# Non-rotated keys and values from a stacked high/low/high latent in fp32r, small constants moved into the norms' tile

## The chip, the cores and the metric

The program runs on one core of one Trainium2 chip. The metric is the device time of one execution in microseconds (us), the median of the runs. TensorE does the matrix products out of SBUF into PSUM, VectorE and ScalarE move and change data in both memories, GpSimd (POOL in the profile) works on SBUF only, and SyncE issues the DMAs. Each engine runs its own instruction stream, and the streams wait for each other on semaphores.

## The reference, cut to what matters

Eight sequences of 512 rows and 256 columns pass through four blocks, each with a layer norm ahead and a residual around it: an attention with three branches, a spiking feed-forward block, a rotary attention with 16 heads of 16, and a product with the signs of a weight. The change touches the first attention, whose first branch takes its keys and values from a latent of 32 columns:

```
ckv    = _rms(x @ w_ckv, g_kvnorm)                        # 512 x 32
k_nope = (ckv @ w_dk_nope).reshape(B, T, 16, 32)          # keys without rotation
v1     = (ckv @ w_dv).reshape(B, T, 16, 32)               # values
k_rope = _rope((x @ w_krope) / 16)                        # one rotated key for all heads
k1     = concat([k_nope, k_rope])                         # 96 per head
scores = x @ w_imp ; idx = top_k(scores, 64)              # rows of the second branch
gate   = softmax((x @ w_gate).mean(over rows))
```

The queries have 96 columns per head, made from a latent of 96 columns; the two other branches take keys and values from x itself and from the 64 rows with the highest scores.

## The kernel before, in words

The program goes through 16 passes: `(0, s)` is the first attention of sequence s, `(1, s)` the second attention of sequence s, in the order (0,0), (0,1), (1,0), (0,2), (1,1) and so on. A pass (0, s) walks over eight pairs of heads, and each pair over twelve units: a unit is a bank of transposed scores, whose exponentials ScalarE takes (`exponentials`, L1857) and whose product with the values TensorE adds into the `outs` banks (`values`, L1218).

Everything else is woven between the units. Each pair g is prepared in seven pieces (`PIECES`: four `qk`, one `nope`, one `val`, one `sel`). For `qk` and `sel`, VectorE multiplies with the rotation's tables (L1423), GpSimd adds (L1961), TensorE transposes (L1112), ScalarE writes the high part and VectorE the low part, the rest that the high part leaves (L1442). `nope` is the product of the keys without rotation (L1092, each pair), of which ScalarE writes the high part and VectorE the low part (L1413) into `K1`; `val` is the values' product (L1095, every second pair). Both read `CKVT`, a tile of 128 rows in float32 whose first 96 rows are zero and whose last 32 hold the transposed latent, against the matching rows of `WQ`. Scores are then three fp32r products of high and low parts (L1181 to L1183). The row maxima are found ahead, from fp32r products at L1147 and VectorE's passes at L1461 and L1464.

`prologue(n, j)` prepares sequence n while the pass (0, n-1) runs: layer norm, transposes, the small projections, VectorE's products for the rotated key (L1571, L1572, in the upper half of the tile `HN`), GpSimd's power and sum (L1945, L2003), the copy of the score row into `ROW` (ScalarE, L1742), its transposes (L1042), the gate's product (L1048), the root mean squares and scaled latents (L1374 to L1586, in the lower half of `HN`), their transposes (L1055), the copies into `NQT` (ScalarE) and `CKVT` (VectorE, L1590), and the ranking of the score row (L1601 to L1615). For the first sequence these steps run with nothing beside them. L1742 is the helper through which ScalarE makes nearly all its copies.

The order of each engine's instructions is fixed when the program is built: `attention_steps` gives each step a time from tables of numbers (`AFTER`, `START`, `PRO`, `MID_A`, `HEADS` and others), in units of one score unit, and sorts. All engines walk through the same sorted list, each doing its own part of a step. `plan_banks` hands the five `work` banks out in that order and counts the readers of each.

Of the kernel before, what the change touches and what calls it, by code (L numbers as in the profile page):

```python
# [11 lines left out]
F32 = mybir.dt.float32  # L12
# [167 lines left out]
def piece_before(g, m, n):  # L180
# [8 lines left out]
AFTER = [dict(pv=2.67, recip=1.87, scale=3.36, late_recip=2.11, late_scale=4.28, scale_gap=0.93, last_recip=1.54, last_scale=3.37, piece=-2.58, gap=0.66, piece_tr=1.99, max=4.98, max_gap=0.31, mt=1.93, rows=-5.38, kr=0.63, val=3.63),  # L189
         dict(odd=3.2, lead=-5.7, lead_odd=4.55, lead_gap=0.79, lead_mt=2.06, pv=3.12, recip=1.78, scale=6.23, last_recip=0.26, last_scale=4.05, max=-0.18, max_gap=1.03, mt=2.45, piece=32.75, gap=1.06, piece_tr=1.93, kr=38.38, val=0.53)]  # L190
# [5 lines left out]
         ("pro_act", 0, 2, 5.29), ("pro_pe", 0, 1, 6.49), ("pro_act", 0, 3, 6.79), ("pro_act", 0, 4, 8.2),  # L196
         ("pro", 0, 4, 8.69), ("pro_pe", 0, 6, 9.1), ("pro_pe", 0, 2, 9.37), ("pro_pe", 0, 3, 11.19),
         ("pro", 0, 5, 11.73), ("pro_act", 0, 5, 12.42), ("kr", 0, 0, 12.93), ("piece", 0, 0, 14.81),
         ("pro_act", 0, 6, 18.69), ("piece", 0, 1, 19.19), ("pro", 0, 6, 20.19), ("piece_tr", 0, 0, 21.05),
         ("piece", 0, 2, 21.32), ("piece_tr", 0, 1, 21.6), ("pro", 0, 7, 22.8), ("piece", 0, 3, 23.83),  # L200
         ("pro", 0, 8, 24.41), ("piece", 0, 4, 24.92), ("piece_tr", 0, 3, 26.89), ("pro", 0, 9, 28.25),
         ("piece", 0, 5, 30.65), ("piece_tr", 0, 4, 30.82), ("pro_pe", 0, 4, 31.22), ("pro_pe", 0, 5, 31.99),
         ("pro", 0, 10, 32.0), ("pro", 0, 11, 37.09), ("pro", 0, 12, 38.82), ("piece", 0, 6, 42.15),
         ("piece_tr", 0, 6, 43.66)]


def tail_steps(at):
# [6 lines left out]
TAIL = [[("wo_early", 3.17), ("wo_last", 5.37), ("tail_add", 0, 5.37), ("tail_add", 1, 6.02),  # L214
         ("tail_var", 0, 7.32), ("tail_var", 1, 8.25), ("tail_ln", 0, 8.6), ("tail_ln", 1, 9.61),
         ("hT", 3, 0, 9.76), ("hT", 3, 1, 10.98), ("sign", 0, 13.37), ("sign", 1, 13.79)],
        [("wo_early", 6.05), ("wo_last", 6.72), ("tail_add", 0, 6.87), ("tail_add", 1, 6.99),
         ("tail_var", 0, 8.23), ("tail_var", 1, 10.23), ("tail_ln", 0, 10.6), ("tail_ln", 1, 10.86),
         ("hT", 3, 0, 12.01), ("hT", 3, 1, 12.37), ("sign", 0, 12.66), ("sign", 1, 13.47)]]
# [5 lines left out]
PRO = [("pro", 0, 58.63), ("pro", 1, 63.32), ("pro_pe", 0, 74.8), ("pro_act", 2, 75.63), ("pro_pe", 1, 76.0),  # L225
       ("pro_act", 3, 76.46), ("pro", 3, 77.3), ("pro_pe", 6, 77.98), ("pro_act", 4, 78.2), ("pro_pe", 2, 80.26),
       ("pro", 4, 83.26), ("pro_pe", 3, 86.16), ("pro_act", 5, 86.54), ("pro", 5, 86.95), ("pro_act", 6, 87.49),
       ("pro", 6, 87.95), ("pro", 7, 88.64), ("pro", 8, 89.15), ("pro", 9, 90.05), ("pro_pe", 4, 93.36),
       ("pro", 10, 94.51), ("pro_pe", 5, 96.73), ("pro", 11, 97.62), ("pro", 12, 104.7)]
# [19 lines left out]
MID_A = [[("ln", 1, 0, 8.17), ("ln", 1, 1, 9.2), ("hT", 1, 0, 9.72), ("hT", 1, 1, 10.6), ("fc", 0, 0, 11.42),  # L249
# [3 lines left out]


MID_B = [("y", 0, 0, 8.85), ("y", 0, 1, 9.75), ("y", 0, 2, 10.47), ("y", 0, 3, 11.45), ("spike", 0, 0, 20.05),
         ("spike", 0, 1, 20.48), ("spike", 0, 2, 21.01), ("spike", 0, 3, 21.23), ("spike", 0, 4, 22.07),
         ("spike", 0, 5, 22.68), ("var", 2, 0, 23.0), ("y", 1, 0, 36.55), ("y", 1, 1, 36.83), ("y", 1, 2, 39.55),
         ("y", 1, 3, 40.63), ("spike", 1, 0, 44.18), ("spike", 1, 1, 45.5), ("spike", 1, 2, 46.17),
         ("spike", 1, 3, 46.23), ("spike", 1, 4, 46.32), ("spike", 1, 5, 46.8), ("var", 2, 1, 47.06),
# [6 lines left out]
         ("fc", 0, 1, 1.52), ("fc", 0, 2, 2.7), ("fc", 0, 3, 3.76), ("y", 0, 0, 5.48), ("y", 0, 1, 6.38),  # L266
         ("y", 0, 2, 6.89), ("y", 0, 3, 7.77), ("spike", 0, 0, 8.65), ("spike", 0, 1, 8.72), ("spike", 0, 2, 8.96),
         ("spike", 0, 3, 9.35), ("spike", 0, 4, 9.8), ("spike", 0, 5, 10.11), ("var", 2, 0, 10.35),
         ("y", 1, 0, 14.35), ("y", 1, 1, 15.12), ("y", 1, 2, 16.02), ("y", 1, 3, 16.66), ("spike", 1, 0, 17.75),
         ("spike", 1, 1, 17.99), ("spike", 1, 2, 18.77), ("spike", 1, 3, 18.79), ("spike", 1, 4, 19.12),  # L270
# [6 lines left out]
          ("heads", 0, 0, 83.62), ("stack", 2, 0, 84.73), ("heads", 1, 0, 85.66), ("stack", 3, 0, 85.93),  # L277
          ("heads", 2, 0, 86.12), ("stack", 0, 1, 86.92), ("heads", 3, 0, 88.26), ("stack", 1, 1, 88.63),
          ("heads", 0, 1, 96.28), ("stack", 2, 1, 96.31), ("heads", 1, 1, 96.88), ("stack", 3, 1, 97.27),
          ("heads", 2, 1, 99.32), ("heads", 3, 1, 100.09), ("v", 0, 100.63), ("v", 1, 106.63)],  # L280
         [("clear", 0, -24.69), ("clear", 1, -19.0), ("stack", 0, 0, -17.57), ("stack", 1, 0, -17.53),
          ("heads", 0, 0, -16.75), ("stack", 2, 0, -16.54), ("heads", 1, 0, -14.38), ("stack", 3, 0, -14.32),
          ("heads", 2, 0, -14.01), ("stack", 0, 1, -13.91), ("heads", 3, 0, -11.88), ("stack", 1, 1, -9.6),
          ("v", 0, -11.26), ("v", 1, -10.97), ("heads", 0, 1, -8.14), ("stack", 2, 1, -7.34),
          ("heads", 1, 1, -5.14), ("stack", 3, 1, -3.83), ("heads", 2, 1, -1.96), ("heads", 3, 1, 3.95)]]


PROJ = [[("proj_early", 5.17), ("proj_last", 7.26), ("proj_add", 0, 7.65), ("proj_add", 1, 7.95),
        ("var", 1, 0, 8.9), ("var", 1, 1, 8.94)],
        [("proj_early", 4.27), ("proj_last", 6.62), ("proj_add", 0, 6.69), ("proj_add", 1, 6.83),  # L290
        ("var", 1, 0, 7.13), ("var", 1, 1, 7.88)]]


def attention_steps(layer, s):

# [153 lines left out]
def plan_banks():  # L449
# [5 lines left out]
    def prologue(n, j):  # L455
        for name in (["hT0", "hT1"], ["small0", "small1"], ["score_cols", "gate"], ["nqT", "ckvT"],
                     ["pos"], ["selT"], ["imp"])[j]:
            work.use(("pro", n, name))
# [103 lines left out]
def build_program(nc, x, w_small, w_imp, w_q, w_nv, w_kw, w_sel, w_proj, g_q, g_kv,  # L562
# [1566 lines left out]
```

## Time and profile before

| | us |
|---|---|
| median of 3 runs | 3019.16 |
| lowest, highest run | 3018.69, 3020.45 |
| profiled execution, its own time | 3020.62 |
| its span | 3018.8 |
| TensorE busy (95% of the span) | 2854.8 |
| VectorE busy (65%) | 1956.6 |
| ScalarE busy (50%) | 1503.6 |
| GpSimd busy (32%) | 957.6 |

The profile is of one execution. Busy times are sums of instructions; matrix products are pipelined, so the time of one is read best from its start to the start of the next. A bracket at the end of a timeline row says how long the engine stood idle ahead of it and which instruction released it. Mean granted TensorE clock is 0.982 of full speed.

### The profile page before, as it was taken

How to read it: one execution, taken by the hardware profiler on the slowest of the kernel's cores; microseconds unless marked ns; L12 is line 12 of the kernel's file. 1: busy time of each engine (PE TensorE's matmuls, PEld its weight loads, DVE VectorE, ACT ScalarE, POOL GpSimd, SP SyncE). 2: the span in 40 equal slices, each digit the busy share in tenths (PEclk: the TensorE clock that was granted, in tenths of full speed). 3: DMA queues.
4: the chain of work that ended last, by engine and by line, in shares of the span. 5: the costliest groups of instructions: out<-in, count | busy, mean ns of one | idle time of the engine just before them, and what ended most of it. 6: DMA issues, size and time to landing. Idle time of an engine off the chain costs nothing. (4 is left out here: it accounts for less than half of the span.)

```text
span 3018.8 us, 53729 instructions
## 1 busy us (share of the span) xinstructions
PE 2854.8 (95%) x18384; PEld 2035.9 (67%) x18384; DVE 1956.6 (65%) x6243; ACT 1503.6 (50%) x3228; POOL 957.6 (32%) x1764
## 2 busy tenths in 40 slices
PE   6999899999999999999999999999999999999987
PEld 4666676667766677666776667766677666776654
DVE  5666656775677656866567766667566775665654
ACT  2554344564445644465444664456544465445543
POOL 1233233432334313333133332334222332233332
PEclk7999999999999999999999999999999999999998
DMA  3111001000110001100101001110111100110000
GB/s 124 34 33 27 25 26 40 25 18 19 41 40 25 25 29 35 33 20 25 38 26 33 25 19 38 33 35 16 30 34 33 31 16 26 33 33 12 16 12 29
DMA packets 58701, 91.44 MB, mean 30 GB/s; under 512 B 19904, under 2 KB 32704, under 8 KB 58176
## 3 DMA queue, kind: packets, MB, share of 16 engines
q1 hardware_dynamic: 58432, 88.01, 9.9%
q8 instruction: 149, 2.44, 0.3%
q14 instruction: 120, 0.98, 0.1%
HBM read 81.68 MB, written 5.24 MB: 29 GB/s over the span
## 5 line engine op out<-in xcount | busy, mean ns | idle before, releaser
L1857 ACT ACTIVATE PR<-work 128x512 f32<-128x512 f32 (+1 forms) x1088 | 642.5, 599 | 710.7 <-PE work L1183 613.3
L1461 DVE CUSTOM_DVE_ANT_0 work<-work,KEEPB 128x128 f32<-128x128 f32 (+3 forms) x1536 | 667.2, 475 | 94.3 <-PE work L1147 93.8
L1972 POOL TENSOR_SCALAR_AFFINE_SELECT PR<-PR 128x256 f32<-128x256 f32 (+1 forms) x960 | 349.9, 369 | 709.6 <-ACT PR L1857 704.1
L1147 PE MATMUL work<-BIG 96*128 96x448 f32 (+8 forms) x1664 | 449.1, 358 | 27.9 <-DVE NMX L1461 15.0
L1181 PE MATMUL work<-BIG 99*128 99x512 f32 (+4 forms) x1152 | 422.8, 367 | 11.2 <-DVE BIG L1442 6.1
L1961 POOL TENSOR_TENSOR TOK<-AB 128x256 f32<-128x256 f32 (+1 forms) x320 | 219.0, 686 | 608.7 <-DVE AB L1423 576.7
L1218 PE MATMUL outs<-PR,ONES 128*32 128x512 f32 (+4 forms) x2304 | 404.9, 458 | 0.0
L1182 PE MATMUL work<-BIG 96*128 96x512 f32 (+4 forms) x1152 | 382.5, 332 | 0.0
L1183 PE MATMUL work<-BIG 96*128 96x512 f32 (+4 forms) x1152 | 380.8, 331 | 0.0
L1147 PEld LDWEIGHTS work<-BIG 96*128 96x128 f32 (+1 forms) x1664 | 267.8, 193 | 157.7 <-issue 78.0
L1442 DVE TENSOR_TENSOR BIG<-work,BIG 96x512 fp32r<-96x512 f32 (+1 forms) x320 | 192.1, 603 | 278.8 <-ACT BIG L1742 278.5
L1742 ACT ACTIVATE BIG<-work 96x512 fp32r<-96x512 f32 (+4 forms) x592 | 334.4, 568 | 38.7 <-PE work L1112 28.0
L1742 ACT ACTIVATE TOK<-work 128x128 f32<-128x128 f32 (+1 forms) x320 | 85.4, 267 | 532.4 <-issue 233.8
L1218 PE MATMUL outs<-PR,VV 128*32 128x512 f32 (+3 forms) x2048 | 337.7, 440 | 3.3 <-POOL PR L1972 3.3
L1181 PEld LDWEIGHTS work<-BIG 99*128 99x128 f32 (+1 forms) x1152 | 210.2, 183 | 161.7 <-issue 110.2
L1089 PE MATMUL work<-WKW,HT 128*128 128x256 f32 x1024 | 275.8, 393 | 0.0
L1423 DVE TENSOR_TENSOR AB<-work,ROPE 128x512 f32<-128x512 f32 (+1 forms) x320 | 201.4, 630 | 102.4 <-PE work L1089 82.9
L1464 DVE TENSOR_REDUCE NMX<-work 128x1 f32<-128x64 f32 (+1 forms) x640 | 170.0, 282 | 124.0 <-PE work L1147 121.7
L1183 PEld LDWEIGHTS work<-BIG 96*128 96x128 f32 (+1 forms) x1152 | 213.1, 185 | 23.7
L1182 PEld LDWEIGHTS work<-BIG 96*128 96x128 f32 (+1 forms) x1152 | 212.6, 185 | 9.9 <-issue 3.4
L1089 PEld LDWEIGHTS work<-WKW,HT 128*128 128x128 f32 x1024 | 195.9, 198 | 16.0
L1112 PE MATMUL work<-ID,TOK 128*96 128x128 f32 x1152 | 180.5, 275 | 18.3 <-ACT VV L1742 8.1
(185 smaller groups left out, 4649.8 us busy)
## 6 DMA issues: line engine op xcount, KB each, us to landing
NRM<-park SPq DMA_DIRECT2D x112, 192.0 KB, 3.1
WKW<-w_kw_dram SPq DMA_DIRECT2D x64, 256.0 KB, 2.7
WSEL<-w_sel_dram SPq DMA_DIRECT2D x64, 256.0 KB, 3.0
R<-park SPq DMA_DIRECT2D x72, 64.0 KB, 2.0
HN<-x_dram SPq DMA_DIRECT2D x8, 512.0 KB, 4.9
X<-x_dram SPq DMA_DIRECT2D x8, 512.0 KB, 3.9
out_dram<-X SPq DMA_DIRECT2D x7, 512.0 KB, 3.2
R<-park SPq DMA_DIRECT2D x16, 192.0 KB, 3.1
```

Source lines behind the costliest of these rows:

```text
L1089: last = mm(ps[:, 192:448], HT0[:, c, t * P:(t + 1) * P], WKW[:, g % 2, c, :], start=(c == 0), stop=(c == NC - 1))
L1147: last = mm(ps[:, col:col + n], q, k, start=(i_mm == 0), stop=(i_mm == len(u["mm"]) - 1))
L1181: mm(out, k[0][0:D0 + 3], q[0][0:D0 + 3], start=(col == 0), stop=False)
L1182: mm(out, k[0][0:D0], q[1][0:D0], start=False, stop=False)
L1183: last = mm(out, k[1][0:D0], q[0][0:D0], start=False, stop=stop)
L1218: last = mm(OB[a][row:row + 32, j * P:T], v, PR[0:rows, slot, col:col + T - j * P], start=(j == 0), stop=(j == 2 or a == A2), skip_group_c ...
L1423: read_work(v.tensor_tensor(rotations(i, rows, heads), src.unsqueeze(1).broadcast_to(shape), ROPE0[0:rows, t, :, :].unsqueeze(2).broadcast ...
L1461: last = v.tensor_tensor_reduce(ps[:, lo:hi], ps[:, lo:hi], KEEPB[:, T - (hi - lo):T], -1.0, -NEG, ALU.add, ALU.min, dst)
L1742: return a.activation(dst, src, ACT.Copy)
L1857: a.activation(PR[0:rows, j % NP, :], ps[0:rows, :], ACT.Exp).then_inc(exp_ready, 1)
L1961: gp.tensor_tensor(dst.rearrange("p h (j d) -> p h j d", j=2), a4, b4[:, :, ::-1, :], ALU.add).then_inc(tok_ready, 1)
L1972: gp.affine_select(blocks, blocks, [[0, len(cols)], [1, P]], ALU.is_ge, 0.0, base=0, channel_multiplier=-1).then_inc(exp_masked, 1)
```

## The change

The transposed latent is kept in `XS`, 96 rows in fp32r: its high part, its low part and its high part again. The weights of the keys and values are kept likewise in `WN` and `WV`, of 96 rows each: high, high, low. One fp32r product of 96 rows then gives high by high, low by high and high by low in one sum. `WN` and `WV` are made at the start: the weights are loaded three times, one below the other, into half of `OT` (`STAGE`), ScalarE copies all rows (rounding to the high part), and VectorE writes the last 32 rows as what is left. For odd pairs the 64 rows that are used lie in the lower half of the bank.

```diff
-        CKVT = sb("CKVT", [P, T])
+        XS = sb("XS", [3 * KVL, T], F32R)
+        WN, WV = sb("WN", [3 * KVL, 512], F32R), sb("WV", [3 * KVL, 512], F32R)
...
-        ROW = sb("ROW", [P, T])[:, :]
+        ROW = HN[:, 2:4, :].rearrange("p t c -> p (t c)")
...
+        GQ, GK, RANKS = NRM[:, 3840:3936], NRM[:, 3936:3968], NRM[:, 3968:4032]
+        COS1, ONES = NRM[:, 4032:4064].rearrange("p (t d) -> p t d", t=NT), NRM[:, 4064:4096]
+        STAGE = OT[0:3 * KVL, 2:4, :].rearrange("p n k -> p (n k)")
+        NV = [(WN[:, :], 0, 512), (WV[:, :], 512, 512)]
...
                 elif what == "nope":
-                    last = mm(ps[:, :], WQ[:, 64 * w:64 * w + P], CKVT[:, :], start=True, stop=True)
+                    if g == 0:
+                        pe.wait_ge(nv_ready, len(NV))
+                    last = mm(ps[:, :], WN[:, P * (w // 2):P * (w // 2 + 1)], XS[:, :], start=True, stop=True)
                 elif what == "val":
                     for t in range(NT):
-                        last = mm(ps[:, t * P:(t + 1) * P], CKVT[:, t * P:(t + 1) * P],
-                                  WQ[:, 512 + 64 * w:512 + 64 * w + P], start=True, stop=True)
+                        last = mm(ps[:, t * P:(t + 1) * P], XS[:, t * P:(t + 1) * P],
+                                  WV[:, P * (w // 2):P * (w // 2 + 1)], start=True, stop=True)
...
+                    for i, (w, c0, n) in enumerate(NV):
+                        dve.wait_ge(nv_high, i + 1)
+                        low = w[2 * KVL:3 * KVL, :]
+                        v.tensor_tensor(low, STAGE[2 * KVL:3 * KVL, c0:c0 + n], low.bitcast(F32), ALU.subtract).then_inc(nv_ready, 1)
...
-                    read(v.tensor_copy(CKVT[QL:P, :], ps[0:KVL, :]), "ckvT")
+                    k, _, _, r, _ = work.of["pro", n, "ckvT"]
+                    dve.wait_ge(work_read[k], r - 1)
+                    read(v.tensor_tensor(XS[KVL:2 * KVL, :], ps[0:KVL, :], XS[0:KVL, :].bitcast(F32), ALU.subtract), "ckvT")
...
-            v.memset(CKVT[0:QL, :], 0.0).then_inc(set_up, 1)
...
-                          5: [("nqT", NQT[0:QL, :], lambda ps: ps[0:QL, :])]}
+                          5: [("nqT", NQT[0:QL, :], lambda ps: ps[0:QL, :])]
+                          + [("ckvT", XS[o:o + KVL, :], lambda ps: ps[0:KVL, :]) for o in (0, 2 * KVL)]}
+                if j == 4:
+                    act.wait_ge(kr_ready, n + 1)
...
+                        if (layer, s) == BEGIN:
+                            act.wait_ge(late_loaded, LATE_LOADED)
+                            for w, c0, n in NV:
+                                copy(w, STAGE[:, c0:c0 + n]).then_inc(nv_high, 1)
...
-       ("pro", 4, 83.26), ("pro_pe", 3, 86.16), ("pro_act", 5, 86.54), ("pro", 5, 86.95), ("pro_act", 6, 87.49),
+       ("pro", 4, 83.26), ("pro_pe", 3, 86.13), ("pro_act", 5, 86.83), ("pro", 5, 87.24), ("pro_act", 6, 88.13),
```

The score row `ROW` now lies in the upper half of `HN`, where the products of the rotated key were, so ScalarE waits for GpSimd's sum of those (`kr_ready`) before it writes. Constants and small tiles move: five into the unused columns of `NRM`, thirteen of a few columns into one tile `SMALL`; the weights of the gate's mean are 64 columns wide in place of 128. The tables of times get new numbers.

ScalarE at the start of the program, where sequence 0 is prepared; L1742 (L1751 after) is the copy helper, `ROW` is the score row (in `HN` after), `BIG` of 64 rows the rotated keys' high part. Before:

```order
L1742 ACTIVATE SM<-work 128x2x195 x2
L1742 ACTIVATE ROW<-work 128x512
L1742 ACTIVATE NQT<-work 96x512
L1742 ACTIVATE BIG<-work 64x2x512
L1742 ACTIVATE TOK<-work 128x4x32
L1742 ACTIVATE VV<-work 128x64
```

And after:

```order
L1751 ACTIVATE SM<-work 128x2x195 x2
L1751 ACTIVATE HN<-work 128x512
L1751 ACTIVATE NQT<-work 96x512
L1751 ACTIVATE XS<-work 32x512 x2
L1751 ACTIVATE BIG<-work 64x2x512
L1751 ACTIVATE WN<-OT 96x512
L1751 ACTIVATE WV<-OT 96x512
L1751 ACTIVATE TOK<-work 128x4x32
```

Four copies are new, two behind the query latent's and two behind the rotated keys'.

VectorE in the pass (0, 1), where sequence 2 is prepared: L1690 (L1700 after) casts the second attention's keys, L1590 copies the latent (L1600 subtracts after), L1601 and L1603 rank the score row, L1477 is a reciprocal of softmax sums. Before:

```order
L1690 CAST BIG<-work 128x4x128 x3
L1590 COPY CKVT<-work 32x512
L1593 TENSOR_REDUCE GM<-GS 128x1
L1601 TENSOR_SCALAR TOK,CG<-ROW,SC 128x512
L1603 SCALAR_TENSOR_TENSOR TOK,CE<-ROW,SC,EARLY 128x512
L1477 RECIPROCAL NRM<-NRM 48x64
L1690 CAST BIG<-work 128x4x128
```

And after:

```order
L1700 CAST BIG<-work 128x4x128 x3
L1600 TENSOR_TENSOR XS<-work,XS 32x512
L1603 TENSOR_REDUCE SMALL<-SMALL 64x1
L1611 TENSOR_SCALAR TOK,SMALL<-HN,SMALL 128x512
L1613 SCALAR_TENSOR_TENSOR TOK,SMALL<-HN,SMALL,EARLY 128x512
L1700 CAST BIG<-work 128x4x128
L1481 RECIPROCAL NRM<-NRM 48x64
```

The latent's step stays where it was and is another operation; the reciprocal and the cast behind it change places.

## Rows read from the trace of the kernel before

**Rows 1.** The page, busy time (share of the span) and instructions of each engine

```profile
PE 2854.8 (95%) x18384; PEld 2035.9 (67%) x18384; DVE 1956.6 (65%) x6243; ACT 1503.6 (50%) x3228; POOL 957.6 (32%) x1764
```

**Rows 2.** Table of windows: stretch, its length, busy us (instructions) per engine, PEclk, DMA

```profile
1763.00:2129.00 366.00, 353.50 (x2297) 252.55 (x2298) 244.51 (x780) 188.01 (x404) 120.16 (x220) 0.99 0.10 29
```

**Rows 3.** TensorE's waits: us in total, times, longest

```profile
PE work L1181 <- ACT ROW L1742: 1.6, 7, 0.2
```

**Rows 4.** Groups by form, TensorE: shapes and count, busy us, mean ns, idle before

```profile
L1092 PE MATMUL work<-CKVT,WQ 128*128 128x512 f32 x128 | 66.0, 597 | 0.0
L1095 PE MATMUL work<-WQ,CKVT 128*128 128x128 f32 x256 | 34.8, 280 | 0.0
```

**Rows 5.** Timeline of TensorE, 189 and 746: start, us, line, operands, shape

```profile
189.37 0.40 PE L1182 MATMUL work<-BIG 96*128 96x512 f32 x1
189.60 0.40 PE L1183 MATMUL work<-BIG 96*128 96x512 f32 x1
...
746.42 1.02 PE L1092 MATMUL work<-CKVT,WQ 128*128 128x512 f32 x2
747.28 0.49 PE L1085 MATMUL work<-WQ,NQT 96*128 96x192 f32 x2
```

**Rows 6.** Timeline of TensorE, 1128 to 1131

```profile
1128.47 1.06 PE L1095 MATMUL work<-WQ,CKVT 128*128 128x128 f32 x8
1129.28 0.42 PE L1181 MATMUL work<-BIG 99*128 99x384 f32 x1
...
1129.96 0.27 PE L1182 MATMUL work<-BIG 96*128 96x128 f32 x1
1130.07 0.28 PE L1183 MATMUL work<-BIG 96*128 96x128 f32 x1
```

**Rows 7.** Timeline of all engines, the start of the program

```profile
20.84 0.60 ACT L1742 ACTIVATE ROW<-work 128x512 f32<-128x512 f32 x1 [1.46 <-PE work L1036]
...
23.19 0.72 POOL L2003 TENSOR_TENSOR KR<-HN 128x256 f32<-128x256 f32 x1
23.26 0.67 DVE L1374 TENSOR_TENSOR NA<-VAR,YP 128x8 f32<-128x8 f32 x1
...
28.47 0.68 DVE L1590 COPY CKVT<-work 32x512 f32<-32x512 f32 x1 [2.03 <-PE work L1055]
...
30.44 1.22 DVE L1433 TENSOR_TENSOR BIG<-work,BIG 64x1024 fp32r<-64x1024 f32 x1 [0.77 <-ACT BIG L1742]
```

**Rows 8.** Timeline of all engines, 577 to 579, preparing sequence 2

```profile
577.27 0.72 POOL L2003 TENSOR_TENSOR KR<-HN 128x256 f32<-128x256 f32 x1
...
577.51 0.59 ACT L1742 ACTIVATE ROW<-work 128x512 f32<-128x512 f32 x1
...
578.16 0.45 PE L1181 MATMUL work<-BIG 99*128 99x384 f32 x1 [0.22 <-ACT ROW L1742]
```

**Rows 9.** Timelines of ScalarE, VectorE and TensorE, 595 to 607, the same sequence

```profile
595.74 0.68 DVE L1590 COPY CKVT<-work 32x512 f32<-32x512 f32 x1 [0.18 <-PE work L1055]
...
597.03 0.62 ACT L1742 ACTIVATE NQT<-work 96x512 f32<-96x512 f32 x1
...
598.39 0.55 DVE L1477 RECIPROCAL NRM<-NRM 48x64 f32<-48x64 f32 x1 [0.33 <-DMA NRM<-NRM]
599.96 0.69 DVE L1690 CAST BIG<-work 128x512 fp32r<-128x512 f32 x1 [1.03 <-PE work L1302]
...
605.96 0.70 DVE L1461 CUSTOM_DVE_ANT_0 work<-work,KEEPB 128x512 f32<-128x512 f32 x1
...
606.77 0.50 PE L1147 MATMUL work<-BIG 128*128 128x384 f32 x2 [0.60 <-DVE NMX L1461]
```

**Rows 10.** Groups by form, VectorE: the subtraction that makes the keys' low part

```profile
L1413 DVE TENSOR_TENSOR BIG<-work,BIG 32x512 fp32r<-32x512 f32 x128 | 87.5, 684 | 160.4 <-ACT BIG L1742 157.9
```

**Rows 11.** Table of windows around the granted clock's fall, columns as in rows 2

```profile
311.00:316.00 5.00, 1.37 (x9) 0.94 (x9) 2.79 (x7) 2.58 (x9) 0.94 (x2) 1.00 0.34 104
316.00:326.00 10.00, 10.00 (x29) 7.80 (x28) 8.97 (x44) 0.39 (x2) 0.72 (x1) 0.51 0.01 2
```

More of the change, by code:

```diff
@@ L200 @@
[L200 to L204, printed above, removed]
+         ("pro_act", 0, 2, 5.29), ("pro_pe", 0, 1, 5.61), ("pro_act", 0, 3, 6.79), ("pro_pe", 0, 6, 7.21),
@@ new lines @@
+         ("pro_act", 0, 4, 8.2), ("pro", 0, 4, 8.69), ("pro_pe", 0, 2, 9.36), ("pro_pe", 0, 3, 9.4),
+         ("pro", 0, 5, 10.15), ("pro_act", 0, 5, 13.6), ("kr", 0, 0, 14.11), ("piece", 0, 0, 15.66),
+         ("pro_act", 0, 6, 18.29), ("piece", 0, 1, 18.79), ("pro", 0, 6, 19.79), ("piece_tr", 0, 0, 20.65),
+         ("piece", 0, 2, 20.92), ("piece_tr", 0, 1, 21.1), ("pro", 0, 7, 22.3), ("piece", 0, 3, 23.33),
+         ("pro", 0, 8, 23.91), ("piece", 0, 4, 24.42), ("piece_tr", 0, 3, 25.26), ("pro", 0, 9, 27.76),
@@ L207, in tail_steps @@
+         ("piece_tr", 0, 4, 29.73), ("pro_pe", 0, 4, 29.83), ("piece", 0, 5, 30.15), ("pro_pe", 0, 5, 30.33),
+         ("pro", 0, 10, 30.72), ("pro", 0, 11, 34.28), ("pro", 0, 12, 34.71), ("piece", 0, 6, 42.03),
+         ("piece_tr", 0, 6, 43.54)]
 def tail_steps(at):
@@ L457, in prologue @@
                      ["pos"], ["selT"], ["imp"])[j]:
-            work.use(("pro", n, name))
+            work.use(("pro", n, name), 3 if name == "ckvT" else 1)
     def attention(layer, s):
@@ L641, in build_program @@
         RSTD = sb("RSTD", [P, 24])
-        SC, CG, CE = sb("SC", [P, NT]), sb("CG", [P, NT]), sb("CE", [P, NT])
-        MF, MB, POS = sb("MF", [P, NT]), sb("MB", [P, NT], BF16), sb("POS", [P, NT])
-        GS, GE, GG = sb("GS", [P, 3]), sb("GE", [P, 3]), sb("GG", [P, 3])
-        GM, GD = sb("GM", [P, 1]), sb("GD", [P, 3])
+        MB = sb("MB", [P, NT], BF16)
+        SMALL = sb("SMALL", [P, 45])
+        widths = [NT] * 5 + [3, 3, 3, 1, 3, 2, 2, 8]
+        SC, CG, CE, MF, POS, GS, GE, GG, GM, GD, NPART, HEAD, MHALF = \
+            (SMALL[:, sum(widths[:i]):sum(widths[:i + 1])] for i in range(len(widths)))
         WB = [ctx.enter_context(nc.psum_tensor(f"work{k}", [P, 512], F32)) for k in range(NWORK)]
@@ L813, in build_program @@
                        (X1[:, :, :].rearrange("p t c -> p (t c)")[:, 0:7 * P], earlier)]
-        late_loads = [(WQ[0:QL, :], w_q), (WQ[QL:P, 0:1024], w_nv), (COS1[:, :, :], cos1), (SIN1[:, :, :], sin1),
+        late_loads = [(WQ[0:QL, :], w_q)] + [(STAGE[KVL * i:KVL * (i + 1), :], w_nv) for i in range(3)] + [
+                      (COS1[:, :, :], cos1), (SIN1[:, :, :], sin1),
                       (WP[:, :, :], w_proj), (WFC[:, :, :], w_fc), (WFP[:, :, :], w_ffp), (WQKV[:, :, :], w_qkv),
@@ L1047, in prologue @@
                     for t in range(NT):
-                        last = mm(ps[:, 0:3], MEANW[:, :], SM[:, t, SM_W - 3:SM_W], start=(t == 0), stop=(t == NT - 1))
+                        last = mm(ps[0:64, 0:3], MEANW[:, :], SM[:, t, SM_W - 3:SM_W], start=(t == 0), stop=(t == NT - 1))
                     last.then_inc(done, 1)
@@ L1412, in piece @@
                         hi, lo = (K1[par][n][ROPE:D0, h, KEEP:] for n in range(2))
-                        read_work(v.tensor_tensor(lo, ps[32 * h:32 * h + 32, :], hi.bitcast(F32), ALU.subtract), use)
+                        o = 64 * (g % 2) + 32 * h
+                        read_work(v.tensor_tensor(lo, ps[o:o + 32, :], hi.bitcast(F32), ALU.subtract), use)
                     return
@@ L1577, in prologue @@
                     ps = filled("gate")
-                    read(v.tensor_copy(GS[:, :], ps[:, 0:3]), "gate")
+                    read(v.tensor_copy(GS[0:64, :], ps[0:64, 0:3]), "gate")
                     rsqrt(powers("pro", n, 1), 2 * NT, RMS_COLS)
@@ L1622, in prologue @@
                     dve.wait_ge(gate_exp, n + 1)
-                    then(v.reciprocal(GD[:, 1:2], GD[:, 0:1]))
+                    then(v.reciprocal(GD[0:64, 1:2], GD[0:64, 0:1]))
                     if n:
@@ L1785, in piece @@
                     for h in range(2):
-                        read_work(copy(K1[g % 2][0][ROPE:D0, h, KEEP:], ps[32 * h:32 * h + 32, :]), use)
+                        o = 64 * (g % 2) + 32 * h
+                        read_work(copy(K1[g % 2][0][ROPE:D0, h, KEEP:], ps[o:o + 32, :]), use)
                     return
```

90 lines of the change are left out of this document (40 added, 50 removed), and 12 rows, old and new, of tables (MID_A, MID_C).

## The prediction, made before the changed kernel was run

> **What bounds the kernel now.** I read the page first: TensorE is busy for 95% of the span [rows 1], so work taken off TensorE can come off the time. The table of windows says how evenly: in a steady sequence (366 us) TensorE is busy for 353.5, VectorE for 244.5, ScalarE for 188.0 [rows 2], so 12.5 us of TensorE are open per sequence, and no other engine is near full over a whole sequence. The list of waits gives the breaks by who ends them. Most of them are short and many; one that matters here, ended by ScalarE's copy of the score row, occurs seven times, once for each sequence but the first [rows 3]. The timeline then shows what the changed products cost and what stands around the new waits. The reader is to take the distance from one start to the next as a product's price, not its duration, since the products are pipelined.
>
> **What the change takes off TensorE.** Two kinds of product change form: the keys without rotation (64 of them, two instructions each, 128x512 in float32) and the values (32 times four products, 256 instructions of 128 columns) [rows 4]. In the timeline a key product starts at 746.42 and its follower at 747.28: 0.86 us. A scores product that already is fp32r with 96 rows, 128 stationary columns and 512 moving ones, the very form that the change gives the keys, goes from 189.37 to 189.60: 0.23 [rows 5]. A key product saves 0.63 us, and 64 save **40.3 us**. The values take from 1128.47 to 1129.28, 0.81 us; an fp32r product of 96x128 on 128 columns takes 0.11 (1129.96 to 1130.07), four of them 0.44 [rows 6]. That saves 0.37 as read; since the last of the eight instructions is cut short in this reading (its follower's start is stamped while it still runs; eight at 0.11 would be 0.88), the other end is 0.44. I take 0.40, and 32 give **12.8 us**. Together 53 us; the bounds are 50 (every key product pays a switch of form where plain float32 stands ahead of it) and 55.
>
> The first thing that one could expect is a different price for the values. The Trainium skill ("TensorE: Matmul & The Clock Gate", Back-to-back issue gap) gives columns over 2.4 GHz plus 2.5 ns as the gap of an isolated product, 56 ns for 128 columns; by it the 32 value groups would save about 7 us more. The trace's 0.11 us speaks against it here, and the same page's section on LDWEIGHTS (columns over 1.2 GHz, 107 ns for 128) fits: with a new stationary operand for each product the load sets the pace. I go by the row.
>
> **What it adds in the steady state.** (a) The score row is now kept in the upper half of the normalised rows' tile, where the two rotated products of the shared key lie until GpSimd has added them. ScalarE's copy of the row therefore waits for that sum. In the trace the sum starts at 577.27 and takes 0.72, the copy starts at 577.51; it would start at about 578.05, 0.5 us later, and TensorE's product at 578.16 was already waiting for just this copy [rows 8]. Behind the waiting copy ScalarE has its exponentials. I charge 0.5 us in seven sequences, **3.5 us**; bounds 0 (the product finds another reason to wait) and 8 (the exponential behind it late as well).
>
> (b) The latent's transpose was copied by VectorE alone at 595.74, 0.68 us. Now ScalarE writes it twice (32x512, rows as long as those of its copy of the query latent, which takes 0.62 [rows 9]) behind that copy, and only then may VectorE subtract. The copy of the query latent starts at 597.03 [rows 9]; the two new ones end at 597.03 + 3 x 0.6 = 598.8, so VectorE ends its part at 599.5 rather than 596.4, 3.1 us later. The order leaves both engines' steps at their places, so this wait stands. Queued behind it on VectorE are the passes over the score row, the cast of the next keys, the reciprocal and then the maxima. Some of it is taken up by VectorE's own idle time there (0.33 us ahead of the reciprocal and 1.03 us ahead of the cast [rows 9]), so about 1.7 us reach the maxima at 605.96, and for these TensorE waits already, 0.60 us at 606.77 [rows 9]. A delay of the maxima is then a delay of TensorE: 1.7 us in the six sequences in which the pattern stands. **10 us**; bounds 0 (ScalarE reaches the copies earlier) and 19 (the whole 3.1). For the other sequence I take nothing. Subtracting instead of copying costs VectorE nothing (0.68 for either [rows 9, 10]).
>
> (c) Moving small constants into one tile and the gate's narrower product change no length that I can find a row for, and ScalarE's 14 more copies as such lie beside TensorE's work: it is busy for 188 of 366 us [rows 2]. If that cover were gone, they would cost 14 x 0.6 = 8 us.
>
> **What it adds at the start.** Here everything hangs on one chain. The row copy at 20.84 would wait for the sum (23.19 + 0.72), so it starts 3.1 us later; transposing the row, the gate's product and VectorE's copies of both follow before the square roots that now start at 23.26 [rows 7]. That is 3 us, less 0.5 for the clearing of the latent's tile that is gone. The split of the latent adds 1.0 (two copies behind the query latent, then the subtraction, against the copy at 28.47 [rows 7]). After the rotated keys' low part at 30.44 VectorE makes the weights' low part, 2 x 0.68 = 1.4 us by the subtraction of as long a row, before it turns to the first pieces [rows 7, 10]. Sum **4.5 us**, bounds 2 and 9. The two extra loads of 128 KB end before ScalarE needs them.
>
> **What does not come through.** TensorE is not the last to be late everywhere. Where a product waits for a chain through ScalarE and VectorE, shortening TensorE's work beneath that chain gives nothing; the open 12.5 us per sequence [rows 2] are such places. I take a tenth of the 53 as lost, **5 us**; at worst a half, 26.
>
> The sum against the profiled execution, 3020.6 us: 3020.6 - 53 + 3.5 + 10 + 4.5 + 5 = 2990.6. That execution is 1.5 us above the median of the runs, so I forecast **2989 us**.
>
> **Rivals.** *All but the products' gain is hidden* (15%): ScalarE reaches the new copies early enough and (a) and (b) find no waiter: 3019 - 53 + 4.5 + 2 = 2972. For it: the table of times was set anew together with the change, and ScalarE is half idle. Against: over these few microseconds ScalarE goes from one instruction to the next, and TensorE waits already. *VectorE's chain becomes the bound* (18%): the whole 3.1 us of (b) reach TensorE, more of the maxima's waits grow, and half the gain is lost beneath other chains: 3019 - 53 + 8 + 19 + 5 + 5 = 3003, or 3008 with 10 lost. *The clock* (4%, slower): at the start of the second sequence's long pass TensorE runs short of work (1.37 of 5 us busy) and the granted clock then falls to 0.51 for the next 10 us, that is from 2.4 to 1.2 GHz [rows 11]. Ten microseconds at half speed cost five. If a lighter TensorE fell out of full clock at further places, each would cost as much: from six of them, 30 us, the change brings nothing, and two in each of seven sequences give 2989 + 70 = 3059. The Trainium skill (same page, HAM oscillation) warns of just this, gaps between products that send the clock back. Against: the waits that I add are 0.5 and 1.7 us, and the waits of that size that the trace has (0.60 at 606.77 [rows 9]) are not what it fell behind. *It does not do what it says* (1%): the new products run as long as float32 ones, and only the costs remain, 3019 + 18 = 3037. The rows of the same form speak against it.
>
> **How the numbers follow.** The forecast's own case has 62% (2980 to 2998, from the bounds of (a), (b) and the start). With the first rival below it and the second above, a range of 2968 to 3007 leaves out about 15%. Within 0.2% (6 us, about what a measurement of this kernel can tell from no change) would need the second rival to go further than I priced it: 3%. Slower by more: the clock and the last rival with the tail of the second, 4%. Faster: 93%.
>
> **What would show it.** In the changed kernel's profile: TensorE's instructions fall by 192, key products take 0.23 and value products 0.11 from start to start; ScalarE's two 32x512 copies stand between the query latent's copy and VectorE's subtraction, with VectorE idle for 2 us or more ahead of it, and TensorE's wait for the maxima behind it is 2 us rather than 0.6; VectorE's first product on a piece starts 4 to 5 us later than now. The forecast is wrong if key products take over 0.3, if VectorE does not wait there, or if the granted clock is low at places where it was not.

## The result, and the profile after

The changed kernel takes 3026.3 us (median of 20 runs, 3018.5 to 3037.6), the kernel before 3019.1 (20 runs, 3014.5 to 3025.6). The ratio is 1.0024, 95% interval 1.0016 to 1.0032: 7 us slower, where 30 us less was forecast. The profiled execution took 3022.7 us, with a span of 3020.8 and a mean granted clock of 0.977 (0.982 before). One run of one experiment below (`sub1_after`) took 3433 us at a granted clock of 0.75; its median and its ratio leave that run out.

The page of the changed kernel answers to [rows 1]: span, then busy time, share and instructions per engine.

```profile
span 3020.8 us, 53375 instructions
PE 2814.1 (93%) x18192; PEld 2011.3 (67%) x18192; DVE 1955.1 (65%) x6244; ACT 1511.1 (50%) x3246; POOL 964.7 (32%) x1764
```

TensorE has 192 instructions fewer, as forecast, and is busy for 41 us less, and yet the span is 2 us longer: 43 us of TensorE have turned into idle time. The table of windows shows it for the sequence of [rows 2], after the change:

```profile
1763.00:2129.00 366.00, 348.43 (x2255) 250.07 (x2254) 240.28 (x765) 186.59 (x402) 119.55 (x217) 0.98 0.10 29
```

The open time of TensorE in this stretch grew from 12.5 to 17.6 us while a sequence still takes 366 us.

The products cost what was said. In TensorE's timeline of the changed kernel, a key product and its follower, then four value products and theirs (columns as in [rows 5, 6]):

```profile
822.72 0.40 PE L1095 MATMUL work<-XS,WN 96*128 96x512 f32 x1
822.96 0.49 PE L1086 MATMUL work<-WQ,NQT 96*128 96x192 f32 x2
...
1133.08 0.64 PE L1098 MATMUL work<-WV,XS 96*128 96x128 f32 x4
1133.56 0.39 PE L1184 MATMUL work<-BIG 99*128 99x384 f32 x1
```

0.24 us and 0.48 us, against 0.86 and 0.81. Over 64 key products and 32 groups of values that is some 50 us. TensorE's waits of the changed kernel (us in total, times, longest) tell where time opened:

```profile
PE work L1150 <- DVE NMX L1465: 20.2, 49, 1.3
PE outs L1221 <- POOL PR L1989: 9.5, 12, 1.1
PE work L1115 <- ACT VV L1751: 9.4, 9, 3.6
PE work L1184 <- ACT VV L1751: 6.2, 12, 0.8
PE work L1184 <- ACT HN L1751: 5.2, 7, 0.8
PE work L1276 <- ACT VV L1751: 2.9, 6, 0.5
PE work L1285 <- DVE BIG L1446: 2.4, 6, 0.4
PE work L1086 <- DVE X L1675: 9.2, 6, 1.5
```

The second line answers to a wait of 3.3 us before, the first to 15.0, the third to 8.1, the fourth to none; the fifth is the score row's, 1.6 before [rows 3]. The sixth and seventh answer to none, the last to 5.4. No line is large. To see where the key products' time went, I matched TensorE's instructions of the two traces one by one and followed how much earlier or later each starts than before, from the start of a key product on (median of the 64; negative is earlier):

```
us after the product's start            0.9    2      4      6      8      10
changed kernel against before (us)     -0.62  -0.63  -0.62  -0.60  -0.01  +0.01
the same behind the 30 value groups    -0.34  -0.37  -0.37  -0.37  -0.38  -0.37
```

At least half of the key products give back their whole gain within 8 us. The values mostly keep theirs over the 10 us that the table covers. One such place, first in the kernel before. Timelines of all engines, bracket: idle time ahead and who ended it.

```profile
98.22 0.59 PE L1092 MATMUL work<-CKVT,WQ 128*128 128x512 f32 x1
98.65 0.49 PE L1085 MATMUL work<-WQ,NQT 96*128 96x192 f32 x2
...
101.19 1.40 DVE L1413 TENSOR_TENSOR BIG<-work,BIG 32x512 fp32r<-32x512 f32 x2 [3.63 <-ACT BIG L1742]
...
102.62 0.69 DVE L1423 TENSOR_TENSOR AB<-work,ROPE 128x512 f32<-128x512 f32 x1
...
103.56 0.22 ACT L1742 ACTIVATE VV<-work 128x64 f32<-128x64 f32 x1
...
103.83 0.50 PE L1181 MATMUL work<-BIG 99*128 99x512 f32 x1
```

And the same place in the changed kernel:

```profile
102.10 0.40 PE L1095 MATMUL work<-XS,WN 96*128 96x512 f32 x1
...
102.37 1.20 ACT L1751 ACTIVATE BIG<-work 3x512 fp32r<-3x512 f32 x2
...
103.59 0.59 ACT L1870 ACTIVATE PR<-work 64x512 f32<-64x512 f32 x1
...
104.20 1.20 ACT L1751 ACTIVATE BIG<-work 32x512 fp32r<-32x512 f32 x2
...
105.50 1.40 DVE L1417 TENSOR_TENSOR BIG<-work,BIG 32x512 fp32r<-32x512 f32 x2 [3.63 <-ACT BIG L1751]
...
106.93 0.69 DVE L1427 TENSOR_TENSOR AB<-work,ROPE 128x512 f32<-128x512 f32 x1
...
107.70 0.28 ACT L1751 ACTIVATE TOK<-work 128x128 f32<-128x128 f32 x1 [2.31 <-issue]
...
107.88 0.22 ACT L1751 ACTIVATE VV<-work 128x64 f32<-128x64 f32 x1
...
108.15 0.50 PE L1184 MATMUL work<-BIG 99*128 99x512 f32 x1 [0.49 <-ACT VV L1751]
```

Read it as one chain: ScalarE copies the maxima (102.37), takes an exponential (103.59), writes the keys' two high parts (104.20); VectorE, idle for 3.63 us, subtracts twice (105.50) and only then turns to the rotation of the next piece (106.93); ScalarE reads the same bank after it (107.70, 107.88), since the kernel has it wait for VectorE's read (`act.wait_ge(work_read[k], r - 2)`; the bracket there, "issue", names no releaser); and TensorE, which needs a bank, starts the next scores (108.15). Before, TensorE reached that point just as the chain ended (103.56 and 0.22, then 103.83). Now it reaches it 0.49 us early and waits.

In the same matching this very wait, for ScalarE's copy into `VV` six microseconds behind the key product, stands behind 19 of the 64 key products (12 at L1184, 6 at L1276, one at L1265). Six more give their gain back at a wait for VectorE's low part (L1285), and six where TensorE waited already, for `X` (5.4 us before, 9.2 now). The rest lose it at other places or keep it past the 10 us of the table, so the one timeline stands for a third of them, and how much is hidden over all 64 has to be measured.

**The theory (A)**: the key products lie beneath chains like this one, so most of their time was never on the path. Its rivals: (B) the added waits of the split and the score row ate the gain; (C) the clock; (D) the new table of times.

### The profile page after: what moved, and what is told of

It is laid out like the page before. It is cut to its first block and busy times, and to the rows that moved or that the text cites. A ratio compares the mean times of both kernels' runs of the same rounds, so it can differ in the third digit from the quotient of the medians.

```text
span 3020.8 us, 53375 instructions
## 1 busy us (share of the span) xinstructions
PE 2814.1 (93%) x18192; PEld 2011.3 (67%) x18192; DVE 1955.1 (65%) x6244; ACT 1511.1 (50%) x3246; POOL 964.7 (32%) x1764
## 5 line engine op out<-in xcount | busy, mean ns | idle before, releaser
L1184 PE MATMUL work<-BIG 99*128 99x512 f32 (+4 forms) x1152 | 424.2, 368 | 21.9 <-ACT VV L1751 6.2
L1221 PE MATMUL outs<-PR,NRM 128*32 128x512 f32 (+4 forms) x2304 | 408.0, 461 | 0.0
L1751 ACT ACTIVATE BIG<-work 96x512 fp32r<-96x512 f32 (+4 forms) x592 | 334.9, 569 | 43.0 <-PE work L1115 34.8
L1751 ACT ACTIVATE TOK<-work 128x128 f32<-128x128 f32 (+1 forms) x320 | 85.7, 268 | 525.0 <-issue 243.8
L1184 PEld LDWEIGHTS work<-BIG 99*128 99x128 f32 (+1 forms) x1152 | 211.7, 184 | 176.8 <-issue 113.4
```

The source lines that it names most:

```text
L1184: mm(out, k[0][0:D0 + 3], q[0][0:D0 + 3], start=(col == 0), stop=False)
L1221: last = mm(OB[a][row:row + 32, j * P:T], v, PR[0:rows, slot, col:col + T - j * P], start=(j == 0), stop=(j == 2 or a == A2), skip_group_c ...
L1751: return a.activation(dst, src, ACT.Copy)
```

## The experiments

Each experiment ran beside the kernel before, 4 to 11 times; times in the text are ratios to it times 3019 us, so that chips can be compared, and the medians stand beside them. A ratio is known to 2 to 5 us to either side, so a difference between two experiments is known to about 5 us.

| kernel | median us | ratio to before, 95% | us against before |
|---|---|---|---|
| changed kernel | 3026.3 | 1.0024 (1.0016, 1.0032) | +7 |
| keys4 | 3030.7 | 1.0046 (1.0032, 1.0059) | +14 |
| oldtab | 3026.7 | 1.0022 (1.0012, 1.0032) | +7 |
| nosplit | 3018.0 | 0.9996 (0.9986, 1.0007) | -1 |
| products | 3006.5 | 0.9959 (0.9946, 0.9973) | -12 |
| vals2 | 3036.8 | 1.0062 (1.0048, 1.0075) | +19 |
| sub1_after | 2995.1 | 0.9926 (0.9912, 0.9939) | -22 |
| sub1_before | 2997.5 | 0.9936 (0.9922, 0.9949) | -19 |
| late32 | 3031.2 | 1.0047 (1.0034, 1.0060) | +14 |
| late3 | 2992.0 | 0.9902 (0.9889, 0.9916) | -30 |
| late3_before | 3002.2 | 0.9937 (0.9925, 0.9950) | -19 |
| late3_products | 2979.7 | 0.9864 (0.9849, 0.9879) | -41 |
| late3_keys4 | 3020.2 | 1.0002 (0.9993, 1.0012) | +1 |
| late3_row | 2985.7 | 0.9890 (0.9876, 0.9903) | -33 |
| cheap | 2988.5 | 0.9895 (0.9880, 0.9911) | -32 |

**keys4.** What does TensorE's time at the key products cost?

```diff
-                    last = mm(ps[:, :], WN[:, P * (w // 2):P * (w // 2 + 1)], XS[:, :], start=True, stop=True)
+                    for _ in range(4):
+                        last = mm(ps[:, :], WN[:, P * (w // 2):P * (w // 2 + 1)], XS[:, :], start=True, stop=True)
```

> The changed kernel, with each of the 64 key products issued four times over (the same product into the same bank, so the result stays): 4 x 0.23 = 0.92 us, which is what the float32 product took before (0.86). Theory A (the key products lie beneath a chain through ScalarE and VectorE that sets when the next piece can go on): the time is within 8 us of the changed kernel's 3026, although TensorE is given 64 x 0.70 = 44 us more. Theory B (TensorE's time counts and the gain was eaten by the added waits of the latent's split and the score row): 3026 + 35 to 44 = 3061 to 3070. Theory C (the clock: a fuller TensorE stays at full clock): not above 3026, with fewer stretches at the low clock.

44 us more for TensorE cost 7 us (4 by the medians), as A has it. C alone would have had it no slower than 3026. The same place in its trace, lines one further down:

```profile
102.80 0.40 PE L1096 MATMUL work<-XS,WN 96*128 96x512 f32 x1
...
105.50 1.40 DVE L1418 TENSOR_TENSOR BIG<-work,BIG 32x512 fp32r<-32x512 f32 x2 [3.63 <-ACT BIG L1752]
...
107.88 0.22 ACT L1752 ACTIVATE VV<-work 128x64 f32<-128x64 f32 x1
...
108.15 0.50 PE L1185 MATMUL work<-BIG 99*128 99x512 f32 x1
```

The last of the four products starts 0.70 us later than the single one did; the subtractions, ScalarE's read and the next scores start at the same hundredth of a microsecond. Only the bracket is gone.

**vals2.** The same question for the values: `for t in [t for t in range(NT) for _ in range(2)]`.

> The changed kernel with each of the 128 value products issued twice: 128 x 0.11 = 14 us more for TensorE, about what the float32 products cost. Theory A (in this form: the chain lies behind key products only, while the values' gain is kept): 3026 + 9 to 14 = 3035 to 3040, three times what 44 us of key products cost. If all of TensorE's small gains are hidden alike: 3026 to 3029.

14 us cost 11.5. The values' time counts where the keys' does not: it is the place, not the size, that hides the keys' gain.

**oldtab.** The changed kernel with the nine tables of times of the kernel before.

> The changed kernel with the tables of times of the kernel before, so that the order of the steps is as it was. Theory A and B: within 6 us of the changed kernel (3020 to 3032), since order was not what kept the gain away. Theory D (the new tables lose what the products gain): 2975 to 2995, about what was forecast.

No difference: D falls.

**nosplit** and **products.** Two removals, one on top of the other:

```diff
-                    dve.wait_ge(work_read[k], r - 1)
-                    read(v.tensor_tensor(XS[KVL:2 * KVL, :], ps[0:KVL, :], XS[0:KVL, :].bitcast(F32), ALU.subtract), "ckvT")
+                    read(v.tensor_copy(XS[0:KVL, :], ps[0:KVL, :]), "ckvT")
...
-        WN, WV = sb("WN", [3 * KVL, 512], F32R), sb("WV", [3 * KVL, 512], F32R)
+        WN = sb("WN", [3 * KVL, 512], F32R)
+        WV = WN
...
-        ROW = HN[:, 2:4, :].rearrange("p t c -> p (t c)")
+        ROW = sb("ROW", [P, T])[:, :]
...
-                if j == 4:
-                    act.wait_ge(kr_ready, n + 1)
```

The first pair of lines is nosplit's, the rest belongs to products alone. Its weights are one tile in place of two, so products has a slightly shorter start for a reason of its own: VectorE's two subtractions for the weights take 0.75 us in products and 1.3 in nosplit.

> The changed kernel without the split of the latent: VectorE copies it once, as before the change, without waiting for ScalarE, and ScalarE's two copies are gone; the other 64 rows of the stacked latent are zero, so keys and values lack their low parts' terms. Theory B: 10 to 25 us below the changed kernel (3001 to 3016), since the wait at the latent is what eats the gain. Theory A: 3 to 8 us below (3018 to 3023).

> The products alone: as the kernel without the split of the latent, and the score row is back in a tile of its own, so ScalarE does not wait for the rotated key's sum; the room for it comes from the values' weights, for which the keys' weights are used (values are wrong, shapes and waits the same). Theory B: 53 us less than the kernel before plus 2 at the start, 2966 to 2972. Theory A: most of the 53 us are hidden even with none of the added waits, 3005 to 3015.

8 us without the split, 11 more without the score row's wait: together the added costs are some 20 us, and the forecast had charged 18 for them. So B, though the costs are real, explains 2 of the 37 us of the miss. The new products alone, with every added cost gone, bring 12 us, where the forecast let 48 of 53 come through; that is 36 of the 37. How the 20 us divide between the split and the row is less certain, since nosplit ran at a lower mean clock (0.9735) than products (0.9776). Nosplit lies at the edge of A's range, products within it, and products is 35 us above B's.

**sub1_after** and **sub1_before.** Take 0.70 us out of the chain, in either kernel:

```diff
-                    dve.wait_ge(work_read[k], r - 2)
-                    for h in range(2):
+                    heads = 2 if g < 2 else 1
+                    dve.wait_ge(work_read[k], r - heads)
+                    for h in range(heads):
```

> The changed kernel with one of VectorE's two subtractions behind each key product left out (the second head's low part is not written after the first two pairs, so its scores are wrong; 0.70 us of VectorE gone, 62 times). Theory A, the chain: in the trace the step behind a key product runs ScalarE's exponential, its two high copies (1.2 us), VectorE's two subtractions (1.4), the rotation, ScalarE's two reads of the same bank, and only then TensorE's next scores. 0.70 us less in it frees at most 62 x 0.62 = 38 us of TensorE that is already early: 3026 - 25 to 38 = 2988 to 3001. If VectorE's part of this chain does not set the pace (theory B or C): 3020 to 3026.

> The kernel before with the same subtraction left out (same reservation). Theory A: there TensorE's longer key product ends just when the chain does, so a shorter chain finds TensorE late itself: 3019 - 0 to 8 = 3011 to 3019. If the subtraction counted by itself in either kernel: about as much less as in the changed one (2981 to 2994).

The changed kernel gains 30 us, as A has it. The kernel before gains 19, where I expected 8 at most. So the chain did not merely keep pace with TensorE before the change: at part of the 62 places it already set it, and a view of TensorE's busy share (95%) did not show that. It also says that 43 us taken from VectorE were worth more there (19 us) than some 50 taken from TensorE (12, in products).

**late32.** A first attempt at a cure, the key products moved away:

```diff
-                t = max(t, free + 0.01 * m)
+                t = max(t, free + 0.01 * m) + 3.2
```

> The changed kernel with each key product and what ScalarE and VectorE do with it moved 3.2 score units later, behind the last rotated piece of its pair, so that its high copies and subtractions no longer stand between the maxima's copies and a rotation. Theory A: the 30 to 38 us come through less what the new place costs: 2988 to 3010. Theory B or C: 3020 to 3032.

A miss: 7 us slower than the changed kernel, where 16 to 38 less was expected. Its waits of TensorE begin with a new line:

```profile
PE work L1150 <- DVE BIG L1446: 28.1, 28, 3.9
```

The maxima's products of the next pair now wait for low parts that queue behind the moved copies (4.9 us in 4 waits in the changed kernel). The list fits the reading that the chain was not shortened but put where the next user comes sooner; no run tested that by itself. Late32 also has the lowest mean clock of all, 0.971 against 0.978; by the line given below for the changed kernel (2.1 us for each 0.001) that is some 14 us, so at the same clock the move might well have been a gain.

**late3, late3_before, late3_products.** The smallest move that lets VectorE use its 3.63 idle us: `+ 0.3` in the same line, which puts the key product just behind the next rotated piece. TensorE, ScalarE and VectorE all follow the list, so the rotation now runs ahead of the subtractions.

> The changed kernel with each key product and what ScalarE and VectorE do with it moved behind the rotated piece that stood directly behind it (0.3 score units later). In the trace VectorE stands idle for 3.6 us ahead of the two subtractions, waiting for ScalarE's high copies, while the product that the rotation behind them reads is complete; now the rotation comes first. Theory A: the rotation and ScalarE's reads of its bank come 3 us earlier, TensorE's next scores wait for neither, and what the key products save comes through: 3026 - 20 to 35 = 2991 to 3006. Theory E (the place of the wait moves: ScalarE's high copies now stand ahead of the high part of the pair's first transposed piece, and TensorE waits there): 3020 to 3032.

> The kernel before with the same move and nothing else. Theory A: the chain was just as long as TensorE's work beneath it there, so the move gives less than in the changed kernel: 3019 - 0 to 15 = 3004 to 3019, and the changed kernel with the move is 10 to 30 us faster than this one. If the hidden gain is not a matter of this chain: the two stand to each other as without the move, the changed one 7 us above.

> The products alone (one copy of the latent by VectorE, low parts missing; the score row in a tile of its own; the keys' weights for the values too) with the same move of the key products. Theory A: the whole of what was priced at first, less a few us: 3019 - 35 to 50 = 2969 to 2984. Theory E: 3000 to 3010, as the products alone without the move.

37 us less than the changed kernel, 29 less than the products alone, and 19 less than the kernel before, which is beyond the 15 that I gave it, as with sub1_before. The changed kernel with the move is 11 us faster than the kernel before with it, where without it it was 7 slower: A's side, at the low edge. But the move brings 19 us without the change too, and against the kernel before with the same move the products alone bring 22 us, where A had the whole price less a few. So the move takes away part of the cover and no more. Timeline of late3 at the same place:

```profile
102.41 0.58 PE L1095 MATMUL work<-XS,WN 96*128 96x512 f32 x1
102.80 0.69 DVE L1427 TENSOR_TENSOR AB<-work,ROPE 128x512 f32<-128x512 f32 x1 [1.63 <-PE work L1090]
...
103.75 0.22 ACT L1751 ACTIVATE VV<-work 128x64 f32<-128x64 f32 x1
...
104.36 0.50 PE L1184 MATMUL work<-BIG 99*128 99x512 f32 x1
...
105.29 1.40 DVE L1417 TENSOR_TENSOR BIG<-work,BIG 32x512 fp32r<-32x512 f32 x2 [1.80 <-ACT BIG L1751]
...
106.74 0.50 PE L1184 MATMUL work<-BIG 99*128 99x512 f32 x1
```

The rotation waits only for its product, ScalarE's read (103.97) ends 1.3 us before the subtractions start, and the scores at 106.74 follow without a bracket.

**late3_keys4.** keys4's edit on top of late3.

> The changed kernel with the key products moved behind the rotated piece, and each of them issued four times over (0.92 us in place of 0.23, 44 us of TensorE in all). Theory A (the chain behind the key product hid it, and the move takes the cover away for most of them): 2992 + 18 to 40 = 3010 to 3032. If the move gave its 34 us for another reason and the key products are as hidden as before: 2992 + 0 to 8 = 2992 to 3000.

The same 44 us that cost 7 without the move cost 30 with it. This bears A out: what hid TensorE's time at the key products was the chain, for with two steps of it exchanged that time counts. It leaves one thing unexplained. Late3_keys4 gives TensorE nearly the same price for its keys as late3_before (0.92 us and 0.86) and takes 20 us longer; the added waits (11 to 20 us) and the keys' 4 us, less what the values gain (about 11), cover 4 to 13 of them.

**late3_row** and **cheap.** What the added waits cost once the chain is out of the way: late3 with the score row in a tile of its own, and late3 with a shorter wait in the split:

```diff
+                          5: [("ckvT", XS[0:KVL, :], lambda ps: ps[0:KVL, :]),
+                              ("nqT", NQT[0:QL, :], lambda ps: ps[0:QL, :]),
+                              ("ckvT", XS[2 * KVL:3 * KVL, :], lambda ps: XS[0:KVL, :].bitcast(F32))]}
```

> The moved version with the score row back in a tile of its own, so ScalarE's copy of it does not wait for the sum of the rotated keys (the keys' weights serve for the values too, to make room; values are wrong, the latent's split stays). By the trace: 3 us at the start and 0.5 us in each of seven sequences, 2992 - 6.5 = 2984 to 2987. If the score row's wait is what the whole of the 12 us hangs on: 2980.

> The moved version, complete, with a shorter wait in the latent's split: ScalarE writes the high part before it turns to the query latent, VectorE waits for this copy alone, and the third part is copied from the first in SBUF. Saved at most 1.2 us of waiting ahead of VectorE's subtraction in each of eight sequences. If the split's wait reaches TensorE as forecast: 2992 - 3 to 10 = 2982 to 2989. If it is covered: 2989 to 2994.

Late3_row has the weights in one tile too. The score row's wait costs 4 us by the ratios, 6 by the medians; the split the remaining 8 or 6 down to late3_products. Of the latter, cheap wins back 2 (3 by the medians), which four runs of it do not tell from nothing. Late3 and cheap compute the whole reference, and both are about 1% faster than either kernel.

## Why the prediction was wrong, point by point

**The new products' price** was right: 0.24 and 0.48 us where 0.23 and 0.44 were forecast, with 192 instructions fewer; the saving is some 50 us in place of 53, the forecast's lower bound. Four value products take 0.48 us, 0.12 each, with a new stationary operand every time. The Trainium skill ("TensorE: Matmul & The Clock Gate", Back-to-back issue gap) gives 56 ns for 128 columns as the gap of an isolated product; its section on LDWEIGHTS, 107 ns for 128 columns, comes nearer to the 120 of this trace.

**(a) the score row** was right by the trace. In the trace of the changed kernel, same sequence as [rows 8]:

```profile
581.39 0.72 POOL L2020 TENSOR_TENSOR KR<-HN 128x256 f32<-128x256 f32 x1
582.15 0.60 ACT L1751 ACTIVATE HN<-work 128x512 f32<-128x512 f32 x1 [0.41 <-POOL KR L2020]
...
582.80 0.44 PE L1184 MATMUL work<-BIG 99*128 99x384 f32 x1 [0.74 <-ACT HN L1751]
```

TensorE's wait grew from 0.22 to 0.74; seven of them hold 5.2 us against 1.6, which is 3.6 where I charged 3.5. The runs say less plainly what it costs with its part of the start, for which 6 were charged: 11 us between nosplit and products, 4 to 6 between late3 and late3_row.

**(b) the split** was right in its mechanism and too dear. VectorE and then the maxima, which answer to [rows 9]:

```profile
603.42 0.68 DVE L1600 TENSOR_TENSOR XS<-work,XS 32x512 fp32r<-32x512 f32 x1 [3.23 <-ACT XS L1751]
...
613.12 0.51 PE L1150 MATMUL work<-BIG 128*128 128x384 f32 x2 [1.27 <-DVE NMX L1465]
```

VectorE waits 3.23 us there (at least 2 was forecast), but TensorE's wait for the maxima rose from 0.60 to 1.27 rather than to 2.3: 0.7 us reach it, not 1.7. Over all sequences the runs give 6 to 9 us for the split with its part of the start; charged were 10 and a part of the start.

**The start** was right: TensorE is 4.5 us later at 60 us, as forecast (the terms given there, 3 less 0.5, 1.0 and 1.4, add up to 4.9). The chain is the one that was named:

```profile
22.04 0.72 POOL L2020 TENSOR_TENSOR KR<-HN 128x256 f32<-128x256 f32 x1
22.79 0.60 ACT L1751 ACTIVATE HN<-work 128x512 f32<-128x512 f32 x1 [4.57 <-POOL KR L2020]
23.53 1.09 PE L1043 MATMUL work<-ID,HN 128*128 128x128 f32 x4 [4.12 <-ACT HN L1751]
```

**"I take a tenth of the 53 as lost"** is the step that failed. I named its mechanism (a product waits for a chain through ScalarE and VectorE, and shortening TensorE's work beneath that chain gives nothing) and then gave it 5 us without looking for the place. The runs put two figures in its place. Taken from the products alone, 53 - 12 = 41 us did not come through, with the effect of the clock in it. Taken from added work, of the 40 us of the keys about 34 were hidden (44 us cost 7, known to about 5: a share of 0.15) and of the 13 us of the values about 2 (14 cost 11.5): some 36 us. Even my worst case, a half, was too low. The rows were there: [rows 10] shows 158 us of VectorE's idle time ahead of just the subtractions behind the key products, and the timeline behind one key product would have shown ScalarE's read ending at 103.78 and TensorE's scores starting at 103.83. "12.5 us open per sequence" was read as the measure of such places. It measures only where TensorE already waits, not where it will wait once it is faster. The rival that came nearest, "VectorE's chain becomes the bound", was mispriced by the same step: its words are that half the gain is lost, but its sum takes off 5 or 10 us. With the half that it names, 26, the sum is 3019 - 53 + 8 + 19 + 5 + 26 = 3024, beyond the range and 2 us from the measured time, though by partly wrong terms: (a) and (b) cost 20 us with the start and not 32.

**The clock**, the rival with 4%, probably took part, and the sign that was named for it (a low clock at places where it was not) is there. The profiled execution of the changed kernel is at the low level (1.2 GHz, half of full) at places where the one before was not. Windows of the changed kernel, then of the kernel before, at the same place in the program:

```profile
1864.00:1873.00 9.00, 8.18 (x62) 5.62 (x60) 4.17 (x16) 4.17 (x9) 1.49 (x5) 1.00 0.48 131
1874.00:1883.00 9.00, 9.00 (x36) 6.66 (x36) 7.10 (x27) 1.79 (x3) 0.97 (x2) 0.50 0.03 6
```

```profile
1863.00:1872.00 9.00, 8.75 (x65) 6.19 (x64) 4.50 (x18) 4.09 (x9) 1.78 (x5) 1.00 0.48 133
1873.00:1882.00 9.00, 8.95 (x62) 6.12 (x62) 8.86 (x30) 1.77 (x3) 1.87 (x3) 1.00 0.00 0
```

TensorE was open for 0.82 of the 9 us ahead of the fall, against 0.25 before, where the clock stayed up; then it did 36 instructions in 9 us rather than 62. Over the 20 runs of the changed kernel the time goes with the mean clock (correlation -0.86; 2.1 us for each 0.001), and over the 51 runs of the kernel before beside the experiments too (-0.81; 1.7 us). The means are 0.9779 and 0.9815. Put to the same clock of 0.980 by these two lines, the kernels take 3021.9 and 3022.3 us: the 7 us by which the change is slower are as large as what the lower clock costs. That is an argument from the scatter of runs; no run here held the clock and changed nothing else. The Trainium skill (same page, HAM oscillation) says that gaps between products send the clock back; the one pair of windows above does not speak against it and does not show it either. If the lines hold for nosplit too (mean clock 0.9735), the 8 us between it and the changed kernel are a lower bound.

With these shares the sum is: 3019, less 6 (keys), less 11 (values), plus 11.5 (score row, split and their start, as they cost in the moved kernels), plus 7 (clock) = 3020.5. With the 20 us that they cost in the kernels without the move it is 3029. The measured 3026 lies between the two, and the intervals of these runs, 2 to 5 us to either side, do not settle more. It stays open where the rest of the gain goes in late3, which is 11 us ahead of late3_before where the products' gain less the added waits would give some 40.

## What to carry to other kernels

Before pricing work taken off the busiest engine, follow the timeline behind it to the next point where that engine needs something from another, and compare the two arrival times: the gain ends at the difference, however full the engine looks over the whole. If they are tied, look in the chain for an engine that stands idle at the head of its queue while a later step of it is ready; one step moved past another was worth 37 us in the changed kernel, five times what the change had lost, and 19 us in the kernel before. Doubling or quadrupling the operation in question costs one line and tells whether more of it counts. It is no full measure of what less of it brings: after the move, 44 us more cost 30, but the products alone, some 50 us less, brought 22.

## What the runs showed that I had not expected

At the place shown, four times the same key product moved the next scores by nothing at all, to 0.01 us: an engine at 93% can have places with half a microsecond of slack and more. VectorE's time counted in the kernel before (19 us for 62 subtractions of 0.70 us), although VectorE is busy for 65% of the span. And the mean clock fell in the order in which TensorE got longer new waits, 0.9815 before, 0.9779 after, 0.971 in late32; but 0.9735 in nosplit, which has fewer added waits than the changed kernel, fits no such order, and I have no reason for it.
